# Mixture-of-slots layer: the dispatch product in two 64-token row tiles that also move an identity

## Chip, cores and metric

One core of a Trainium2 chip. The time is device microseconds of one execution of the program, as the median over several runs. The engines are TensorE (PE; its weight loads are PEld), VectorE (DVE), ScalarE (ACT), GpSimd (POOL) and SyncE (SP), which here only issues transfers.

## The reference, cut to what matters

The input x is 32 sequences of 64 tokens of 256 numbers. A cross attention (32 heads of 8) is added to x first. Then comes the part that is changed, a soft mixture of 16 experts with 128 slots each. The reference computes it as:

```python
x_ln = (x - mean) / jnp.sqrt(var + LN_EPS) * gamma + beta
x_n = _l2norm(x_ln, -1) * scale
logits = jnp.einsum('bnd,des->bnes', x_n, mu_n)
dispatch = jax.nn.softmax(logits, axis=1)
combine = jax.nn.softmax(logits.reshape(B, N, E * S), axis=-1)
slot_in = jnp.einsum('bnd,bnes->besd', x_ln, dispatch)
h = gelu(jnp.einsum('besd,edh->besh', slot_in, W1) + b1[None, :, None, :])
slot_out = jnp.einsum('besh,ehd->besd', h, W2) + b2[None, :, None, :]
out = jnp.einsum('bsd,bns->bnd', slot_out.reshape(B, E * S, D), combine)
```

Everything is float32.

## The kernel before, in words

**Tiling.** The 2048 tokens are 16 tiles of 128 tokens, so a tile is two sequences (b = 0 on partitions 0 to 63, b = 1 on 64 to 127). The attention runs over all 16 tiles first, then the expert layer over all 16. Each engine has its own program, and they meet at semaphores: `wait_ge(sem, n)` waits until a counter has reached n, `then_inc` raises it. An engine works through its list strictly in the written order, so the order of the calls in `ffn_step` of each engine's block is the schedule. The last attention tiles and the first steps of the layer are written out by hand.

**One step of the expert layer, tile s.** The product with W1 is taken before the dispatch, on the tokens, since both are linear: xw = x_ln W1 + b1, 16 experts times 64 columns, with a column of ones for the sum of the exponentials. The calls on TensorE (`ffn_step`, L1168) are:

- `expand` (L1114): xw, 1024 columns in two banks, with split operands: `mm3` (L913) makes three products of float32r halves (lines L915 to L917), so all rows of slot logits, expand and contract carry these three lines. VectorE's `xw_copy` (L809) adds b1 and puts the two sequences at different columns of `xw`, the rest of which is zero: four additions on 64 partitions.
- `transpose_e` (L1123): 16 transposes of the exponentials `eb` (tokens x slots) into banks 6, 7, 0, 1. `eT_copy` moves them to `eT`: groups 0 and 2 on ScalarE (L542), groups 3 and 1 on VectorE (L819), for the last tile all four on ScalarE.
- `transpose_xl` (L1093): the next tile's normalised input. VectorE's `xlT_copy` (L802) splits it into two halves.
- `dispatch` (L1131): for each expert `eb.T @ xw`, a 128-row product with 2 x 65 columns. A float32 product is two passes in the trace. The experts go in six groups, `HG`, of three (the last of one), one bank each, three banks in turn (`HB`); group i + 3 waits until group i has been read. VectorE's `hidden` (L834) takes the reciprocal of the sums and multiplies.
- `slot_logits` (L1100) of tile s + 1, in four banks of 512 columns. ScalarE's `slot_exps` (L534) makes `eb` of them.
- `combine` (L1144): a small transpose of the sums of exponentials, then 32 products of 64 columns in two column tiles, Gelu'd hidden values times `eT`, in two halves. ScalarE's `gT_high` (L553) casts each half, and VectorE's `gT_low` (L848) subtracts to get the low half.
- `contract` (L1159): the product with W2, which waits for these. VectorE's `finish` (L856) scales, adds x, and the tile is stored.

**ScalarE's order** (`ffn_step`, L559): `eT_copy` of two groups, `gelus` (three activations on two groups each, L548), `slot_exps` of tile s + 1, `gT_high`, then the sum of squares of tile s + 2. Gelu and Exp have different activation tables, so each step has two table loads, which appear at the lines of the Gelu (L551) and of the Exp (L539).

**VectorE's order** (`ffn_step`, L864): `clamp`, `xw_copy`, `xlT_copy`, `hidden` with the copies of `eT`, `center` of tile s + 2, `gT_low`, `sums` of tile s + 1, `finish`.

GpSimd does the affine part of the normalisation and the row scales (L417, L424). Before the layer it fills the constant parts of `xw` (L407 to L411).

Of the kernel before, what the change touches and what calls it, by code (L numbers as in the profile page):

```python
# [14 lines left out]
F32 = mybir.dt.float32  # L15
# [5 lines left out]
P = 128  # L21
# [13 lines left out]
HC = HID + 1  # L35

# [8 lines left out]
def build(nc, x, ctx_in, pos, Wq, Wkv, Wout, bout, gamma, beta, mu, scale, W1, b1, W2, b2, out):  # L45
    ctx = ExitStack()
    with ctx:
# [67 lines left out]
        rh = sb("rh", P, EXPERTS, 2)  # L115
# [3 lines left out]
        bank = [ctx.enter_context(nc.psum_tensor(f"bank{i}", [P, BANK], F32)) for i in range(8)]  # L119
# [83 lines left out]
        xw_step = sem("xw_step")  # L203
# [3 lines left out]
        eT_filled = sem("eT_filled")  # L207
        eT_act = sem("eT_act")
        eT_dve = sem("eT_dve")
# [25 lines left out]
        PER = BANK // (2 * HC)  # L235
# [4 lines left out]
        LB = (0, 1, 2, 5)  # L240
        HB = (4, 5, 3)
# [17 lines left out]
        XW = EXPERTS * 2 * HC  # L259
        xw = w12f[:, 0:XW].rearrange("p (e c) -> p e c", c=2 * HC)  # L260
# [3 lines left out]
        xl = xc  # L264

# [53 lines left out]
        def _(pool):  # L319
# [131 lines left out]
        def _(act):  # L451
# [101 lines left out]
            def gT_high(t):  # L553
                for c in range(2):
                    act.wait_ge(g_filled, t * 2 + c + 1)
                    a.copy(gT[0][:, 4 * c:4 * c + 4, :].rearrange("p a b -> p (a b)"), bank[(6, 3)[c]][:])\  # L556
# [28 lines left out]
        def _(dve):  # L585
# [216 lines left out]
            def xlT_copy(t):  # L802
                dve.wait_ge(xlT_filled, t + 1)
                v.tensor_copy(flat(xlT[0]), bank[2][:, 0:DIM]).then_inc(xlT_split, 1)
                dve.wait_ge(xlT_split, t + 1)
                v.tensor_tensor(flat(xlT[1]), bank[2][:, 0:DIM], flat(xlT[0]).bitcast(F32), ALU.subtract)\  # L806
# [12 lines left out]
            def eT_copy(t, gr):  # L819
                dve.wait_ge(eT_filled, t * 4 + gr + 1)  # L820
                v.tensor_copy(eT[:, 4 * gr:4 * gr + 4, :].rearrange("p a b -> p (a b)"), bank[(6, 7, 0, 1)[gr]][:])\
                    .then_inc(eT_dve, 1)
# [11 lines left out]
            def hidden(t, last):  # L834

                for i, gr in enumerate(HG):
                    if i == 3 and not last:
                        eT_copy(t, 3)
                    n, e0 = len(gr), gr[0]
                    dve.wait_ge(h_filled, t * len(HG) + i + 1)  # L840
                    src = bank[HB[i % 3]][:, 0:n * 2 * HC].rearrange("p (n b c) -> p n b c", b=2, c=HC)
                    v.reciprocal(rh[:, e0:e0 + n, :], src[:, :, :, HID]).then_inc(rh_done, 1)
                    dve.wait_ge(rh_done, t * len(HG) + i + 1)
                    v.tensor_tensor(hb[:, e0:e0 + n], src[:, :, :, 0:HID],  # L844
                                    rh[:, e0:e0 + n, :].unsqueeze(3).broadcast_to([P, n, 2, HID]),
                                    ALU.mult).then_inc(hn_ready, 1)

            def gT_low(t):  # L848
                dve.wait_ge(esT_filled, t + 1)
                v.tensor_copy(esT[:], bank[7][0:EXPERTS, 0:P]).then_inc(esT_ready, 1)  # L850
                for c in range(2):
                    high, low = (h[:, 4 * c:4 * c + 4, :].rearrange("p a b -> p (a b)") for h in gT)
                    dve.wait_ge(gT_split, t * 2 + c + 1)
                    v.tensor_tensor(low, bank[(6, 3)[c]][:], high.bitcast(F32), ALU.subtract).then_inc(gT_ready, 1)  # L854
# [9 lines left out]
            def ffn_step(s, p, last=False, ahead=True):  # L864
# [5 lines left out]
                hidden(s, last)  # L870
                if not last:
                    eT_copy(s, 1)
# [17 lines left out]
            residual(TILES - 2, 3)  # L890
            dve.wait_ge(wb_loaded, 64)
            dve.wait_ge(xw_const, 2)
# [16 lines left out]
        def _(pe):  # L909
# [183 lines left out]
            def transpose_xl(t, p):  # L1093
                pe.wait_ge(xl_ready, t + 1)
                wait(pe, xw_ready, t * 4 - 2)
                for k in range(KD):
                    m = nc.tensor.transpose(bank[2][:, k * P:(k + 1) * P], xl[:, p, k * P:(k + 1) * P], ident[:])
# [16 lines left out]
            def expand(t):  # L1114

                pe.wait_ge(e_ready, t * 4 + 3)
# [6 lines left out]
            def transpose_e(t):  # L1123
                for gr in range(4):
                    pe.wait_ge(e_ready, t * 4 + gr + 1)
                    for i in range(4):
# [108 lines left out]
```

## Time and profile before

| | |
|---|---|
| Median of 3 runs | 569.59 us |
| Runs | 567.27 to 569.8 us |
| Span of the profiled execution | 560.9 us |
| TensorE busy | 501.4 us, 89% |
| TensorE weight loads | 406.3 us, 72% |
| VectorE busy | 422.3 us, 75% |
| ScalarE busy | 290.3 us, 52% |
| GpSimd busy | 148.5 us, 26% |

The profiled execution has no time of its own beside its span; the runs lie 6.4 to 8.9 us above that span, which is what surrounds the first and last recorded instruction. In the page, busy shares are averages over an attention half (to about 245 us) and an expert half (from there on). A row of a timeline has a start, a length in us, the engine, the line, the operation and the tiles out<-in; a number in square brackets is the idle time of the engine just before, with what ended it.

### The profile page before, as it was taken

What the parts mean: (1) busy time and instruction counts of PE and PEld (TensorE: products, weight loads), DVE (VectorE), ACT (ScalarE), POOL (GpSimd) and SP (SyncE); (2) the same over time, 40 slices, a digit from 0 to 9 for tenths busy, and PEclk for the clock granted to TensorE, in tenths of its full rate; (3) what the DMA queues carried; (4) which work ended last, traced back from release to release, by engine and by line L of the source; (5) the groups of instructions that cost most, each with busy time, mean ns of one, the idle gap of its engine ahead of it and who ended that gap; (6) DMA issues with size and microseconds to landing.
All of it is one profiled execution on the core that took longest, in us unless ns stands there. A gap on an engine that the chain in (4) does not pass through costs nothing.

```text
span 560.9 us, 14312 instructions
## 1 busy us (share of the span) xinstructions
PE 501.4 (89%) x5544; PEld 406.3 (72%) x5544; DVE 422.3 (75%) x823; ACT 290.3 (52%) x537; POOL 148.5 (26%) x248
## 2 busy tenths in 40 slices
PE   0676999987797878889999999999999999999997
PEld 0444666654565555668888898898889889888986
DVE  5788998896799999856866686686668668666854
ACT  1363656664354646635455635745563574556344
POOL 4329211518363832311211212111121211112100
PEclk9868999999698989999999999999999999999999
DMA  6500000006000200000000000000000000000000
GB/s 188 197 6 6 8 6 7 8 1 160 6 6 5 62 0 1 4 1 1 11 11 2 11 9 9 0 9 9 0 9 9 9 0 9 9 0 9 11 11 11
DMA packets 15665, 11.65 MB, mean 21 GB/s; under 512 B 7040, under 2 KB 15120, under 8 KB 15376
## 3 DMA queue, kind: packets, MB, share of 16 engines
q1 hardware_dynamic: 15632, 11.18, 6.7%
q8 instruction: 25, 0.41, 0.3%
q14 instruction: 8, 0.07, 0.0%
HBM read 9.08 MB, written 2.10 MB: 20 GB/s over the span
## 4 chain that ended last, share of the span: by engine, by line
PE 75%; DVE 16%; ACT 3%; issue 2%; SPq 1%; DMA 1%; POOL 0%; DVEq 0%; ACTq 0%
PE bank L915 13%; PE bank L917 12%; PE bank L916 12%; PE bank L1140 10%; PE bank L1155 6%; PE bank L1127 5%; DVE qkr L664 4%; PE bank L965 4%; PE bank L980 4%; PE bank L994 3%; DVE rc L694 3%; PE bank L1014 2%; DVE mx L677 2%; PE bank L1161 2%; DVE pb L682 2%
## 5 line engine op out<-in xcount | busy, mean ns | idle before, releaser
L462 ACT ACTIVATE pb<-pb 128x512 f32<-128x512 f32 x64 | 39.4, 632 | 64.2 <-DVE pb L682 64.2
L545 ACT COPY mu_raw<-bank 128x512 f32<-128x512 f32 x34 | 19.7, 588 | 98.4 <-PE bank L1127 98.4
L1140 PE MATMUL bank<-w_raw,eb 128*128 128x130 f32 x512 | 60.2, 275 | 1.0 <-DVE w_raw L815 0.9
L1140 PEld LDWEIGHTS bank<-w_raw,eb 128*128 128x128 f32 x512 | 58.5, 190 | 1.5 <-DVE w_raw L815 1.4
L551 ACT ACTIVATE pb<-pb 128x768 f32<-128x768 f32 (+1 forms) x48 | 37.1, 774 | 40.1 <-DVE pb L844 40.1
L915 PE MATMUL bank<-mun_h,xlT_l 128*128 128x512 f32 x128 | 51.9, 405 | 0.2 <-DVE xlT_l L806 0.2
L844 DVE TENSOR_TENSOR pb<-bank,rh 128x384 f32<-128x384 f32 x96 | 49.3, 513 | 3.3
L980 PEld LDWEIGHTS bank<-ident,pb 128*128 128x128 f32 x256 | 31.3, 156 | 27.7 <-issue 25.0
L980 PE MATMUL bank<-ident,pb 128*128 128x128 f32 x256 | 45.9, 309 | 5.8 <-ACT vb L479 3.6
L917 PE MATMUL bank<-mun_h,xlT_h 128*128 128x512 f32 x128 | 50.6, 395 | 0.0
L916 PE MATMUL bank<-mun_l,xlT_h 128*128 128x512 f32 x128 | 50.5, 395 | 0.0
L815 DVE TENSOR_TENSOR w_raw<-bank,mu_raw 64x512 f32<-64x512 f32 x64 | 44.1, 689 | 6.4 <-PE bank L917 4.9
L677 DVE TENSOR_REDUCE mx<-bank 128x8 f32<-128x512 f32 x64 | 41.0, 682 | 9.3 <-PE bank L965 9.2
L539 ACT ACTIVATE eb<-bank,nshift,rn 128x512 f32<-128x512 f32 x64 | 44.9, 777 | 3.2 <-PE bank L917 1.6
L965 PE MATMUL bank<-kT,qT 32*64 32x256 f32 x512 | 45.1, 443 | 0.0
L854 DVE TENSOR_TENSOR gT_l<-bank,gT_h 128x512 fp32r<-128x512 f32 x32 | 22.1, 692 | 26.8 <-ACT gT_h L556 26.8
L420 POOL TENSOR_TENSOR xc<-xc,mu_raw 128x256 f32<-128x256 f32 x16 | 11.8, 735 | 115.0 <-DVE xc L792 115.0
L334 POOL TENSOR_TENSOR sm<-sm,mhalf 128x1 f32<-128x1 f32 x16 | 8.8, 549 | 123.6 <-DVE sm L799 123.6
L682 DVE TENSOR_TENSOR pb<-bank,mx 128x512 f32<-128x512 f32 x64 | 40.9, 679 | 0.0
L466 ACT COPY pT<-bank 128x512 f32<-128x512 f32 x64 | 35.7, 594 | 7.9 <-PE bank L980 7.7
L850 DVE COPY esT<-bank 16x128 f32<-16x128 f32 x16 | 4.4, 278 | 45.8 <-PE bank L1148 45.8
L915 PE MATMUL bank<-w_h,gT_l 128*128 128x256 f32 x128 | 37.1, 290 | 0.0
(156 smaller groups left out, 1261.2 us busy)
## 6 DMA issues: line engine op xcount, KB each, us to landing
mu_raw<-in_L_ffn_mu SPq DMA_DIRECT2D x1, 2048.0 KB, 12.8
out<-w_raw SPq DMA_DIRECT2D x16, 128.0 KB, 1.7
xa<-in_x SPq DMA_DIRECT2D x1, 1536.0 KB, 8.4
ctile<-in_ctx SPq DMA_DIRECT2D x16, 64.0 KB, 1.9
w_raw<-in_L_ffn_W SPq DMA_DIRECT2D x2, 512.0 KB, 5.3
w_raw<-in_L_ffn_W SPq DMA_DIRECT2D x1, 1024.0 KB, 9.1
xa<-in_x SPq DMA_DIRECT2D x1, 512.0 KB, 3.6
mu_raw<-in_L_ffn_b SPq DMA_DIRECT2D x1, 512.0 KB, 3.1
```

The source lines that it names most:

```text
L462: a.activation(pb[:, p, gr], pb[:, p, gr], ACT.Exp, scale=HD ** -0.5).then_inc(p_ready, 1)
L539: a.activation(eb[:, 4 * c:4 * c + 4, :].rearrange("p a b -> p (a b)"), bank[LB[c]][:], ACT.Exp, scale=rn[:, p:p + 1], bias=nshift[:]).the ...
L677: v.reduce_max(mx[:, gr, :], bank[gr][:].rearrange("p (h k) -> p h k", k=SEQ), AX.X)\
L682: v.tensor_tensor(pb[:, p, gr], bank[gr][:].rearrange("p (h k) -> p h k", k=SEQ), mx[:, gr, :].unsqueeze(2).broadcast_to([P, 8, SEQ]), ALU ...
L815: v.tensor_tensor(xw[rows, 8 * c:8 * c + 8, b * HC:b * HC + HID], bank[2 + c][rows].rearrange("p (e h) -> p e h", h=HID), b1b[rows, 8 * c: ...
L844: v.tensor_tensor(hb[:, e0:e0 + n], src[:, :, :, 0:HID], rh[:, e0:e0 + n, :].unsqueeze(3).broadcast_to([P, n, 2, HID]), ALU.mult).then_inc ...
L915: mm(o, a[1], b[0], start=first, stop=False)
L916: mm(o, a[0], b[1], start=False, stop=False)
L917: return mm(o, a[0], b[0], start=False, stop=last)
L965: m = mm(bank[g][cols, 256 * half:256 * half + 256].rearrange("p (j n) -> p j n", j=4), qT[rows, half, cols], kT[rows, half, :, cols], sta ...
L980: m = nc.tensor.transpose(bank[6 + gr % 2][:, i * P:(i + 1) * P], pb[:, p, gr, 2 * i:2 * i + 2, :].rearrange("p h k -> p (h k)"), ident[:])
L1140: m = mm(bank[HB[i % 3]][:, n * 2 * HC:(n + 1) * 2 * HC], eb[:, e, :], xw[:, e, :], start=True, stop=True)
```

## The change

The identity is put beside the 65 columns of each expert: `xw` becomes 16 x 129 columns, where row t holds xw, a one, and a one at column t of its own sequence. The dispatch of an expert becomes two products of 64 rows each, one for each sequence, into two neighbouring banks: columns 0 to 64 give the hidden sums, columns 65 to 128 the transposed exponentials. `transpose_e` and its copies go. ScalarE copies the transposed part of each group (six copies of up to 384 elements), and VectorE reads the rest of the pair of banks after it. The banks of the slot logits, of the next tile's transposes and of combine move with that, and so do some waits. `PER` is still 3, so there are six groups as before.

```diff
-        rh = sb("rh", P, EXPERTS, 2)
+        rh = sb("rh", P, 2, EXPERTS)
-        PER = BANK // (2 * HC)
+        PER = BANK // XC
-        LB = (0, 1, 2, 5)
-        HB = (4, 5, 3)
+        LB = (2, 3, 0, 1)
+
+        HB = (6, 4, 0)
+        def pair(i, n):
+
+            b0 = HB[i % 3]
+            return psum[:, b0:b0 + 2, 0:n * XC].rearrange("p b (n c) -> p b n c", c=XC)
...
@@ GpSimd
-            g.memset(w12f[:, 0:XW], 0.0).then_inc(xw_step, 1)
-            pool.wait_ge(xw_step, 1)
+            g.memset(xw[:, :, HID:HC], 1.0).then_inc(xw_const, 1)
             for b in range(2):
-                g.memset(xw[64 * b:64 * b + 64, :, b * HC + HID:b * HC + HC], 1.0).then_inc(xw_const, 1)
-            pool.wait_ge(xw_const, 2)
+                pool.wait_ge(xw_const, b + 1)
+                rows = slice(64 * b, 64 * b + 64)
+                g.tensor_copy(xw[rows, :, HC:XC], ident[rows, rows].unsqueeze(1).broadcast_to([64, EXPERTS, SEQ]))\
+                    .then_inc(xw_const, 1)
+            pool.wait_ge(xw_const, 3)
...
@@ ScalarE
-            def eT_copy(t, groups):
-                for gr in groups:
-                    act.wait_ge(eT_filled, t * 4 + gr + 1)
-                    a.copy(eT[:, 4 * gr:4 * gr + 4, :].rearrange("p a b -> p (a b)"),
-                           bank[(6, 7, 0, 1)[gr]][:]).then_inc(eT_act, 1)
+            def eT_copy(t):
+
+                for i, gr in enumerate(HG):
+                    n, e0 = len(gr), gr[0]
+                    act.wait_ge(h_filled, t * len(HG) + i + 1)
+                    a.copy(eT[:, e0:e0 + n, :].rearrange("p n (b k) -> p b n k", b=2),
+                           pair(i, n)[:, :, :, HC:XC]).then_inc(eT_ready, 1)
             def ffn_step(s, p, last=False, sums=True):
-                eT_copy(s, range(4) if last else (0, 2))
+                eT_copy(s)
                 gelus(s)
...
@@ VectorE
                 for c in range(2):
                     dve.wait_ge(xw_filled, t * 2 + c + 1)
-                    for b in range(2):
-                        rows = slice(64 * b, 64 * b + 64)
-                        v.tensor_tensor(xw[rows, 8 * c:8 * c + 8, b * HC:b * HC + HID],
-                                        bank[2 + c][rows].rearrange("p (e h) -> p e h", h=HID),
-                                        b1b[rows, 8 * c:8 * c + 8, :], ALU.add).then_inc(xw_ready, 1)
+                    v.tensor_tensor(xw[:, 8 * c:8 * c + 8, 0:HID], bank[2 + c].rearrange("p (e h) -> p e h", h=HID),
+                                    b1b[:, 8 * c:8 * c + 8, :], ALU.add).then_inc(xw_ready, 1)
-            def hidden(t, last):
+            def hidden(t):
                 for i, gr in enumerate(HG):
-                    if i == 3 and not last:
-                        eT_copy(t, 3)
                     n, e0 = len(gr), gr[0]
-                    dve.wait_ge(h_filled, t * len(HG) + i + 1)
+                    dve.wait_ge(eT_ready, t * len(HG) + i + 1)
+                    src = pair(i, n)
...
@@ TensorE
-            def dispatch(t):
-
-                pe.wait_ge(xw_ready, t * 4 + 4)
+            def dispatch(t, last, first=False):
+
+                pe.wait_ge(xw_ready, t * 2 + 2)
                 for i, gr in enumerate(HG):
-                    if i == 0:
+                    if i == 1:
                         wait(pe, yo_ready, t)
+                        if first:
+                            pe.wait_ge(x1_ready, TILES)
+                    if i == 2:
+                        pe.wait_ge(e_ready, t * 4 + 4)
+                        if not last:
+                            pe.wait_ge(xlT_ready, t + 2)
                     if i >= 3:
                         pe.wait_ge(hn_ready, t * len(HG) + i - 2)
                     for n, e in enumerate(gr):
-                        m = mm(bank[HB[i % 3]][:, n * 2 * HC:(n + 1) * 2 * HC], eb[:, e, :], xw[:, e, :],
-                               start=True, stop=True)
+                        for b in range(2):
+                            rows = slice(64 * b, 64 * b + 64)
+                            m = mm(bank[HB[i % 3] + b][:, n * XC:(n + 1) * XC], eb[rows, e, :], xw[rows, e, :],
+                                   start=True, stop=True)
                     m.then_inc(h_filled, 1)
...
@@ slot_logits: the waits
-                    if c < 2:
-                        wait(pe, (eT_act, eT_dve)[c], (t * 2, t * 2 - 1)[c])
-                    elif c == 3:
-                        wait(pe, hn_ready, (t - 1) * len(HG) + 5)
+                    if c == 2:
+                        wait(pe, hn_ready, t * len(HG))
@@ combine: the waits
                 pe.wait_ge(es_ready, t + 1)
-                pe.wait_ge(eT_act, t * 2 + (4 if last else 2))
-                pe.wait_ge(eT_dve, t * 2 + (0 if last else 2))
+                pe.wait_ge(hn_ready, t * len(HG) + len(HG))
@@ ffn_step
                 if not expanded:
                     expand(s)
-                transpose_e(s)
-                if expanded:
-                    pe.wait_ge(x1_ready, TILES)
                 if not last:
                     transpose_xl(s + 1, 1 - p)
-                dispatch(s)
+                dispatch(s, last, first=expanded)
```

In `expand` the wait for the Exps of the tile is now for two of them instead of three, in `transpose_xl` it is for all four, and `xlT_copy` reads bank 1.

## Rows read from the trace of the kernel before

**Rows 1.** The page: busy time by engine, and the chain that ended last, by engine.
```profile
PE 501.4 (89%) x5544; PEld 406.3 (72%) x5544; DVE 422.3 (75%) x823; ACT 290.3 (52%) x537; POOL 148.5 (26%) x248
...
PE 75%; DVE 16%; ACT 3%; issue 2%; SPq 1%; DMA 1%; POOL 0%; DVEq 0%; ACTq 0%
```

**Rows 2.** The chain in order of time: start, us, what (dispatch of four tiles).
```profile
253.29 3.85 PE bank L1140 x32
...
273.20 3.85 PE bank L1140 x32
...
293.08 3.58 PE bank L1140 x32
...
528.44 3.58 PE bank L1140 x32
```

**Rows 3.** Timeline, TensorE, 405 to 423 us: start, us, engine, line, op, out<-in.
```profile
405.84 0.39 PE L915 MATMUL bank<-w_h,xlT_l 128*128 128x512 f32 x1
...
408.63 1.91 PE L1127 MATMUL bank<-ident,eb 128*128 128x128 f32 x16
...
410.38 0.38 PE L1097 MATMUL bank<-ident,xc 128*128 128x128 f32 x2
...
410.60 3.75 PE L1140 MATMUL bank<-w_raw,eb 128*128 128x130 f32 x32
...
414.10 0.48 PE L915 MATMUL bank<-mun_h,xlT_l 128*128 128x512 f32 x1
...
419.98 2.09 PE L1155 MATMUL bank<-mu_raw,pb 128*64 128x64 f32 x64
...
422.62 0.38 PE L915 MATMUL bank<-w_h,gT_l 128*128 128x256 f32 x1
```

**Rows 4.** Timeline, ScalarE, the same step.
```profile
410.75 1.28 ACT L551 ACT_TABLE_LOAD   x1
...
413.11 0.84 ACT L551 ACTIVATE pb<-pb 128x768 f32<-128x768 f32 x1 [1.07 <-DVE pb L844]
...
416.19 0.63 ACT L551 ACTIVATE pb<-pb 128x512 f32<-128x512 f32 x1 [0.25 <-DVE pb L844]
...
416.84 1.28 ACT L539 ACT_TABLE_LOAD   x1
...
418.13 2.79 ACT L539 ACTIVATE eb<-bank,nshift,rn 128x512 f32<-128x512 f32 x4
...
421.18 0.59 ACT L556 CAST gT_h<-bank 128x512 fp32r<-128x512 f32 x1 [0.26 <-PE bank L1155]
```

**Rows 5.** Timeline, VectorE, the same step.
```profile
407.43 2.85 DVE L815 TENSOR_TENSOR w_raw<-bank,mu_raw 64x512 f32<-64x512 f32 x4 [0.24 <-PE bank L917]
...
412.29 0.19 DVE L842 RECIPROCAL rh<-bank 128x6 f32<-128x6 f32 x1
...
412.51 0.56 DVE L844 TENSOR_TENSOR pb<-bank,rh 128x384 f32<-128x384 f32 x1
...
412.99 0.18 DVE L842 RECIPROCAL rh<-bank 128x6 f32<-128x6 f32 x1
...
421.80 0.69 DVE L854 TENSOR_TENSOR gT_l<-bank,gT_h 128x512 fp32r<-128x512 f32 x1 [1.43 <-ACT gT_h L556]
```

**Rows 6.** Line L493: count, ns min/median/max, first and last start.
```profile
L493 ACT CAST xT_h<-bank x16: 479/484/485, 14.3 to 212.3; 128x384 fp32r<-128x384 f32 x16
```

**Rows 7.** Timeline, TensorE, one group of attention logits.
```profile
203.31 0.66 PE L965 MATMUL bank<-kT,qT 32*64 32x256 f32 x8
```

**Rows 8.** Timeline of the last tile, TensorE and VectorE.
```profile
547.67 3.81 PE L1140 MATMUL bank<-w_raw,eb 128*128 128x130 f32 x32
...
548.61 0.20 DVE L842 RECIPROCAL rh<-bank 128x6 f32<-128x6 f32 x1 [1.03 <-PE bank L1140]
...
552.41 2.08 PE L1155 MATMUL bank<-mu_raw,pb 128*64 128x64 f32 x64 [0.82 <-ACT pb L551]
```

**Rows 9.** Timeline, VectorE, before the first dispatch.
```profile
250.39 2.84 DVE L815 TENSOR_TENSOR w_raw<-bank,mu_raw 64x512 f32<-64x512 f32 x4
```

More of the change, by code:

```diff
@@ L35 @@
 HC = HID + 1
+XC = HC + SEQ
 def wait(eng, sem, value):
@@ L114, in build @@
         rs = sb("rs", P, 2, 2)
-        rh = sb("rh", P, EXPERTS, 2)
+        rh = sb("rh", P, 2, EXPERTS)
         gT = split("gT", P, EXPERTS // 2, P)
         esT = sb("esT", EXPERTS, P)
-        bank = [ctx.enter_context(nc.psum_tensor(f"bank{i}", [P, BANK], F32)) for i in range(8)]
+        psum = ctx.enter_context(nc.psum_tensor("psum", [P, 8, BANK], F32))
+        bank = [psum[:, i, :] for i in range(8)]
         x_loaded = [sem("x_loaded0"), sem("x_loaded1")]
@@ L258, in build @@
         w12f = flat(w12_raw)
-        XW = EXPERTS * 2 * HC
-        xw = w12f[:, 0:XW].rearrange("p (e c) -> p e c", c=2 * HC)
+        XW = EXPERTS * XC
+        xw = w12f[:, 0:XW].rearrange("p (e c) -> p e c", c=XC)
         yo = w12f[:, XW:XW + 2 * DIM].rearrange("p (a d) -> p a d", d=DIM)
@@ L555, in gT_high @@
                     act.wait_ge(g_filled, t * 2 + c + 1)
-                    a.copy(gT[0][:, 4 * c:4 * c + 4, :].rearrange("p a b -> p (a b)"), bank[(6, 3)[c]][:])\
+                    a.copy(gT[0][:, 4 * c:4 * c + 4, :].rearrange("p a b -> p (a b)"), bank[6 + c][:])\
                         .then_inc(gT_split, 1)
             def ffn_step(s, p, last=False, sums=True):
-                eT_copy(s, range(4) if last else (0, 2))
+                eT_copy(s)
                 gelus(s)
@@ L853, in gT_low @@
                     dve.wait_ge(gT_split, t * 2 + c + 1)
-                    v.tensor_tensor(low, bank[(6, 3)[c]][:], high.bitcast(F32), ALU.subtract).then_inc(gT_ready, 1)
+                    v.tensor_tensor(low, bank[6 + c][:], high.bitcast(F32), ALU.subtract).then_inc(gT_ready, 1)
             def finish(t, p):
@@ L869, in ffn_step @@
                     xlT_copy(s + 1)
-                hidden(s, last)
-                if not last:
-                    eT_copy(s, 1)
+                hidden(s)
                 if ahead:
@@ L889, in _ @@
             normalise(TILES - 2)
-            residual(TILES - 2, 3)
+            residual(TILES - 2)
             dve.wait_ge(wb_loaded, 64)
-            dve.wait_ge(xw_const, 2)
+            dve.wait_ge(xw_const, 3)
             sums(0, 0)
@@ L1094, in transpose_xl @@
                 pe.wait_ge(xl_ready, t + 1)
-                wait(pe, xw_ready, t * 4 - 2)
+                wait(pe, e_ready, t * 4)
                 for k in range(KD):
-                    m = nc.tensor.transpose(bank[2][:, k * P:(k + 1) * P], xl[:, p, k * P:(k + 1) * P], ident[:])
+                    m = nc.tensor.transpose(bank[1][:, k * P:(k + 1) * P], xl[:, p, k * P:(k + 1) * P], ident[:])
                 m.then_inc(xlT_filled, 1)
@@ L1121, in expand @@
                     m.then_inc(xw_filled, 1)
[L1123 to L1126, printed above, removed]
-                        m = nc.tensor.transpose(bank[(6, 7, 0, 1)[gr]][:, i * P:(i + 1) * P], eb[:, 4 * gr + i, :],
-                                                ident[:])
-                    m.then_inc(eT_filled, 1)
-            def dispatch(t):
-                pe.wait_ge(xw_ready, t * 4 + 4)
+            def dispatch(t, last, first=False):
+                pe.wait_ge(xw_ready, t * 2 + 2)
                 for i, gr in enumerate(HG):
-                    if i == 0:
+                    if i == 1:
                         wait(pe, yo_ready, t)
+                        if first:
[4 more added lines that the diff above has]
+                            pe.wait_ge(xlT_ready, t + 2)
                     if i >= 3:
@@ L1139, in dispatch, with combine @@
                     for n, e in enumerate(gr):
-                        m = mm(bank[HB[i % 3]][:, n * 2 * HC:(n + 1) * 2 * HC], eb[:, e, :], xw[:, e, :],
-                               start=True, stop=True)
+                        for b in range(2):
+                            rows = slice(64 * b, 64 * b + 64)
+                            m = mm(bank[HB[i % 3] + b][:, n * XC:(n + 1) * XC], eb[rows, e, :], xw[rows, e, :],
+                                   start=True, stop=True)
                     m.then_inc(h_filled, 1)
-            def combine(t, last):
+            def combine(t):
                 pe.wait_ge(es_ready, t + 1)
-                pe.wait_ge(eT_act, t * 2 + (4 if last else 2))
-                pe.wait_ge(eT_dve, t * 2 + (0 if last else 2))
-                nc.tensor.transpose(bank[7][0:EXPERTS, 0:P], es[:], ident[:]).then_inc(esT_filled, 1)
+                pe.wait_ge(hn_ready, t * len(HG) + len(HG))
+                nc.tensor.transpose(bank[5][0:EXPERTS, 0:P], es[:], ident[:]).then_inc(esT_filled, 1)
                 for c in range(2):
@@ L1170, in ffn_step @@
                     expand(s)
-                transpose_e(s)
-                if expanded:
-                    pe.wait_ge(x1_ready, TILES)
                 if not last:
                     transpose_xl(s + 1, 1 - p)
-                dispatch(s)
+                dispatch(s, last, first=expanded)
                 if not last:
                     slot_logits(s + 1)
-                combine(s, last)
+                combine(s)
                 contract(s)
```

29 lines of the change are left out of this document (10 added, 19 removed).

## The prediction, made before the changed kernel was run

> **What bounds the kernel now.** I read the page first. TensorE is busy for 89% of the span and carries 75% of the chain that ended last [rows 1]: less work on TensorE is worth something, unless the order of the other engines takes its place. The chain in order of time then gives the pace of the second half: the dispatch product of a tile starts every (528.44 − 293.08) / 12 = 19.61 us [rows 2]. The question is what sets these 19.61 us after the change.
>
> The timeline of one step on TensorE [rows 3], counted from the start S of the dispatch (410.60), reads: dispatch 3.50, slot logits of the next tile and the small transpose to 9.38, combine, contract from 12.02 (422.62), expand from 14.85 (405.84 plus a period) to 17.64 (408.63 plus a period), then 1.97 us of transposes, 16 of the exponentials and 2 of the next tile, until the next dispatch. There is hardly a gap: TensorE sets the pace.
>
> ScalarE beside it [rows 4] is what I would have the reader look at. Its order is fixed: copies of transposed exponentials, Gelu table, three Gelus, Exp table, four Exps, then the casts of the combined product. The Gelu table is loaded at S + 0.15, while the engine waits for its first input, which comes at S + 2.51. The last Exp ends at S + 10.32 (418.13 + 2.79), and the first cast starts at S + 10.58: the whole queue has 0.26 us to spare. VectorE [rows 5] follows each cast with a subtraction, and TensorE's contract starts 0.13 us after the first of those.
>
> Times here are of the profiled execution, span 560.9. The median of the runs is 569.59, 8.7 us more; I add my difference to it. About 0.5% (2.8 us) is what a measurement can tell from no change.
>
> **The change, part by part.** Removed on TensorE: 16 transposes a tile. They take 410.60 − 408.63 less 0.22 for the two that stay, 1.75 us a step [rows 3]; if nothing else moved, 28 us in 16 steps.
>
> Their cover is lost. While they ran, VectorE added the bias for the dispatch (four 64-partition additions, 2.85 us, 0.71 each [rows 5], the last ending 0.32 before the dispatch). Now there are two additions on 128 partitions. The width in partitions should cost nothing, since the row of 384 elements on 128 partitions takes 0.56; I take 0.70 for each. The second begins 0.24 after expand's end, as the third of the four does now, so the dispatch starts at 0.24 + 0.70 + 0.06 = 1.00 us after expand, not 1.97. The 0.06 is from 253.23, where the additions of the first tile end, to 253.29 [rows 2, 9]. Of the 1.75 us, 0.97 are left.
>
> The dispatch itself: 32 passes of 130 columns took 3.50, 0.109 each [rows 3]. Now each expert has two 64-row products of 129 columns, four passes, in two banks. The trace has no 64-row tile. The nearest row is the 32-row, 64-column product: eight passes of 256 columns in 0.66 us [rows 7], where eight in series at the rate of the dispatch would take 1.7. Combine, in two column tiles, shows it too: 64 passes of 64 columns in 2.09 [rows 3], in series 3.4. So tiles run side by side. Lower bound 0.107 for a pair of passes, upper bound 0.22 (in series); I take 0.112, near the rows with tiles. A group of three experts: 0.67.
>
> The ordering now costs: ScalarE copies the transposed half of each pair of banks first, and only then may VectorE take the reciprocals and multiply. A group is seen by its reader 0.94 after its first pass (548.61 − 547.67) [rows 8]. The copy has 384 elements of two banks; a cast of 384 out of one took 0.48 [rows 6]; bounds 0.38 and 0.59, those of 256 and of 512 elements (the cast of 512 took 0.59, and the Gelus of 768 and 512 differ by 0.21 for 256 elements [rows 4]). Then reciprocal to product 0.22 and product 0.56, one group each 0.70 [rows 5]. From S: group 1 filled 0.94, copied 1.42, normalised 2.23; groups 2 and 3 at 2.93 and 3.63. There are three pairs of banks, so groups 4, 5, 6 start at 2.29, 2.99, 3.69. The last group is one expert: filled 4.18, its copy waits for that of group 5 (3.93 to 4.41) and ends at 4.57 (estimate: 0.48 less 0.21, so 0.27 for 128 elements). TensorE is done with the dispatch at 3.91 instead of 3.50; the stalls come from VectorE's 0.70 a group.
>
> Other waits that the change adds, taken at nothing: group 3 waits for the split of the next tile's transposed input (VectorE, two operations of 0.42 behind the bias additions, ready near S + 0.9, wanted at 1.34); the third slice of slot logits waits for the last normalised group (5.6, wanted at 6.8). Behind VectorE's new waits for ScalarE stand the centring of the tile after next and the subtractions; those are wanted at 12, and VectorE no longer has the two copies of 0.68. No DMA is issued in another order.
>
> Now ScalarE's queue, which is the point of my forecast. All six copies stand before the Gelus. The table load, which used to fall into the wait, comes behind the last copy: 4.59 to 5.87. Gelus (0.84, 0.84, 0.63, each beginning 0.11 before the other ends, as the four Exps in 2.79 do) 5.88 to 7.98. Table 8.00 to 9.28. Exps to 12.07 in full, the last starting at 11.30, and the first cast can start at 11.96. Subtraction 12.58 to 13.27 and contract at 13.40, where it is 12.02 now: **+1.38**. TensorE has combined half a tile by 3.91 + 0.1 + 5.88 + 1.20 = 11.09, so it waits.
>
> Sum of a step: 13.40 + contract 2.83 + expand 2.79 + 1.00 = **20.02 against 19.61, +0.41**.
>
> Rule against row: each table load in the trace takes 1.28 and the first Exp starts 0.01 behind it (416.84, 418.13) [rows 4]. The Trainium skill, page "ScalarE: Activation LUTs", section "What ACT_TABLE_LOAD costs", counts a drain of about 1.38 us on top for every switch. The trace of before does not show it, neither at the Exp load (which begins 0.02 behind the last Gelu) nor behind it. By the page, both switches now being exposed, the step would be some 2.8 us longer, near 22.8; I go by the row.
>
> At the front: two additions of 0.71 fewer before the first dispatch [rows 9], −1.4; the first step, which also has the variances of the last tiles on VectorE, goes from 19.91 (253.29 to 273.20) [rows 2] to about 20.1, +0.2. On GpSimd one memset of 2080 columns is replaced by one of 16 and two copies of the identity, long before the first dispatch; bound ±0.5, hidden by the attention tiles, taken as 0. Then 14 steps (273.20 to 547.67) of +0.41: +5.7. At the end combine starts at the end of the second Gelu plus 0.06, at 7.51, where it is 552.41 − 547.67 = 4.74 after the dispatch [rows 8]: +2.8. Sum −1.4 + 0.2 + 5.7 + 2.8 = +7.3: span 568.2, **time 576.9**.
>
> **The rivals.** (a) *Faster, 0.12.* The Gelu table is loaded ahead of the copies, where ScalarE idles, as the copies need no table of their own. Price: 1.28 off ScalarE's chain. It decides as soon as the chain is more than 0.87 (11.96 − 11.09) shorter: then TensorE sets the pace again at 20.02 − 0.87 = 19.15 a step. 15 × −0.46, −1.4 at the front, +2.8 − 1.28 at the end: −6.8, 562.8. Against it: in [rows 4] the load stands behind the copies, right in front of the Gelus.
>
> (b) *No difference, 0.20.* ScalarE's chain is 0.3 to 0.6 shorter than I have it (copies at 0.42, quicker releases, more overlap between Gelus): 570 ± 2.5. The step's two losses then just eat the 0.97.
>
> (c) *Tiles in series, 0.05.* Each expert takes four passes, 0.45 us; a group 1.34, so the last copy ends near 7.70, not 4.57. +3.1 a step, about 627. The rows of tiled products speak against it. The Trainium skill, page "TensorE: Matmul & The Clock Gate", section "LDWEIGHTS (loading the stationary operand)", has a load cost by its columns and not its rows: that gives four full loads an expert where there were two, and would bring this case if loads of different row tiles did not overlap. In the row at 203.31 eight loads and products fit in 0.66.
>
> (d) The forecast, ScalarE's queue as the bound: 0.63, 573 to 582.
>
> **The numbers.** Slower is (d) and (c), 0.68; same 0.20; faster 0.12. The likeliest case gives 576.9. The low end takes in (a), 562; the high end the bounds above: copies at 0.59 with a slower release (+0.2 a step) and pairs of passes at 0.12 (+0.1), 584. Case (c) is left out. The likeliest case alone: 573 to 582.
>
> **What would show it.** Right: no row for the transposes; a dispatch of about 3.9 us with short idles on VectorE's products; period near 20.0; Gelu table load at S + 4.6; the first cast following the last Exp with no idle, and TensorE idle for about 1.1 us before contract "until VectorE's subtraction", and about 0.8 before the dispatch, until the bias addition. Wrong: a Gelu load before S + 1 (case a); idle of ScalarE before the cast on TensorE (b or a); dispatch passes 0.11 apart one by one, 7 us in all (c); a gap between a table load and its neighbours (the page's drain).

## The result and the profile after

The changed kernel took 577.08 us (median of 4 runs, 574.23 to 578.23), the kernel before 568.43 beside it, a ratio of 1.0137 with a 95% interval of 1.0094 to 1.018. A second series gave 578.01 against 567.82, ratio 1.0201 (1.0172 to 1.023). The ratios and intervals are the ones on record; they need not equal the quotient of two medians (here 1.0152 and 1.0179). The change is slower by 1.4 to 2%.

The spans of the two profiles differ by more (576.0 against 560.9) than the medians do. Most of the excess lies ahead of the part that was changed: in the first profile of the kernel before, the attention ran with a mean granted clock of 0.93, in the profile after with 0.91, and the first dispatch came 3.6 us later where 1.4 us earlier was predicted. Experiment 5 comes back to this. One sentence on the time before was wrong: the 6.4 to 8.9 us between that profile's span and the runs are not only what surrounds the recorded instructions. In the eleven profiled executions since, whose own times are on record, the time is 1.8 to 2.4 us above the span (578.23 over 576.0 here). By that the first profile caught an execution of some 563 us (an estimate), faster than any of the runs beside it.

The page after, busy time and the chain that ended last, which answer to [rows 1]:

```profile
PE 494.7 (86%) x5800; PEld 389.4 (68%) x5800; DVE 383.8 (67%) x761; ACT 305.1 (53%) x599; POOL 149.0 (26%) x248
...
PE 46%; ACT 22%; DVE 21%; issue 8%; SPq 1%; DMA 1%; POOL 0%; ACTq 0%; DVEq 0%
```

TensorE has lost 6.7 us of busy time: 10.5 in the expert half (303.9 to 293.5), while the attention half at its lower clock took 3.7 more (197.5 to 201.2). The chain that ended last is now only 46% TensorE; ScalarE, 3% before, has 22%. The bound has moved. The chain in order of time (start, us, what), which answers to [rows 2]:

```profile
256.84 0.96 PE psum L1135 x12
...
276.95 0.96 PE psum L1135 x12
...
558.35 0.96 PE psum L1135 x12
```

The period is (558.35 − 276.95) / 14 = 20.10 us, where it was 19.61. One step on TensorE, as in [rows 3]: start, us, engine, line, op, and in brackets the idle time before and what ended it.

```profile
417.60 4.22 PE L1135 MATMUL psum<-w_raw,eb 64*128 64x129 f32 x64 [0.57 <-DVE w_raw L822]
421.75 0.50 PE L912 MATMUL psum<-mun_h,xlT_l 128*128 128x512 f32 x1
...
427.65 2.08 PE L1149 MATMUL psum<-mu_raw,pb 128*64 128x64 f32 x64
...
431.03 0.39 PE L912 MATMUL psum<-w_h,gT_l 128*128 128x256 f32 x1 [0.67 <-DVE gT_l L853]
...
433.97 0.40 PE L912 MATMUL psum<-w_h,xlT_l 128*128 128x512 f32 x1
...
436.76 0.38 PE L1094 MATMUL psum<-ident,xc 128*128 128x128 f32 x2
437.71 0.49 PE L1135 MATMUL psum<-w_raw,eb 64*128 64x129 f32 x4 [0.56 <-DVE w_raw L822]
```

Here 417.60 is the start S of the dispatch. It lasts to 421.75, 4.15 us. The two gaps are the ones to read: 0.67 us before contract, until VectorE's subtraction (beside the weight load's own wait of 1.1), and 0.56 before the next dispatch, until the bias addition. ScalarE in the same step, as in [rows 4]:

```profile
418.58 0.48 ACT L554 COPY mu_raw<-psum 128x384 f32<-128x384 f32 x1 [7.55 <-PE psum L1135]
...
421.62 0.65 ACT L554 COPY mu_raw<-psum 128x384 f32<-128x384 f32 x2 [0.21 <-PE psum L1135]
422.29 1.28 ACT L560 ACT_TABLE_LOAD   x1
423.58 2.10 ACT L560 ACTIVATE pb<-pb 128x768 f32<-128x768 f32 x3
425.70 1.28 ACT L546 ACT_TABLE_LOAD   x1
427.00 2.79 ACT L546 ACTIVATE eb<-psum,nshift,rn 128x512 f32<-128x512 f32 x4
429.66 1.08 ACT L565 CAST gT_h<-psum 128x512 fp32r<-128x512 f32 x2
```

From 421.62 to the end of the casts there is no idle time at all: the last two of the six copies, table, Gelus, table, Exps, casts. In [rows 4] the Gelus and the cast that are shown had an idle time in brackets; now none has. VectorE, as in [rows 5]:

```profile
430.29 1.29 DVE L853 TENSOR_TENSOR gT_l<-psum,gT_h 128x512 fp32r<-128x512 f32 x2 [2.25 <-ACT gT_h L565]
...
436.96 0.69 DVE L822 TENSOR_TENSOR w_raw<-psum,mu_raw 128x512 f32<-128x512 f32 x1 [0.70 <-PE psum L914]
```

The subtraction now waits 2.25 us for a cast, not 1.43. The second bias addition (436.96, 128 partitions) takes 0.69, like one of 64 partitions before, and starts 0.20 after expand's end.

### The profile page after: what moved, and what is told of

Read it like the earlier page. It is cut to its first block, busy times and chain, and to the rows that moved or that the text cites. A ratio compares the mean times of both kernels' runs of the same rounds, so it can differ in the third digit from the quotient of the medians.

```text
span 576.0 us, 14783 instructions
## 1 busy us (share of the span) xinstructions
PE 494.7 (86%) x5800; PEld 389.4 (68%) x5800; DVE 383.8 (67%) x761; ACT 305.1 (53%) x599; POOL 149.0 (26%) x248
## 4 chain that ended last, share of the span: by engine, by line
PE 46%; ACT 22%; DVE 21%; issue 8%; SPq 1%; DMA 1%; POOL 0%; ACTq 0%; DVEq 0%
PE psum L912 8%; PE psum L1135 7%; ACT eb L546 7%; PE psum L914 7%; PE psum L913 7%; PE psum L962 4%; PE psum L977 4%; DVE qkr L673 4%; ACT pb L560 4%; PE psum L991 3%; ACT L560 3%; DVE rc L703 3%; ACT mu_raw L554 2%; DVE w_raw L822 2%; PE psum L1011 2%
## 5 line engine op out<-in xcount | busy, mean ns | idle before, releaser
L554 ACT COPY mu_raw<-psum 128x384 f32<-128x384 f32 x96 | 41.0, 445 | 141.0 <-PE psum L1135 141.0
L1135 PE MATMUL psum<-w_raw,eb 64*128 64x129 f32 x1024 | 66.6, 279 | 11.6 <-DVE w_raw L822 10.7
L1135 PEld LDWEIGHTS psum<-w_raw,eb 64*128 64x128 f32 x1024 | 60.4, 187 | 18.7 <-DVE w_raw L822 14.7
L912 PE MATMUL psum<-mun_h,xlT_l 128*128 128x512 f32 x128 | 52.2, 408 | 0.2 <-DVE xlT_l L815 0.2
L977 PE MATMUL psum<-ident,pb 128*128 128x128 f32 x256 | 47.0, 314 | 6.1 <-ACT vb L486 3.8
L843 DVE TENSOR_TENSOR pb<-psum,rh 128x384 f32<-128x384 f32 x96 | 49.2, 513 | 3.3
L914 PE MATMUL psum<-mun_h,xlT_h 128*128 128x512 f32 x128 | 50.6, 395 | 0.0
L913 PE MATMUL psum<-mun_l,xlT_h 128*128 128x512 f32 x128 | 50.5, 395 | 0.0
L546 ACT ACTIVATE eb<-psum,nshift,rn 128x512 f32<-128x512 f32 x64 | 44.9, 777 | 3.3 <-PE psum L914 1.6
L962 PE MATMUL psum<-kT,qT 32*64 32x256 f32 x512 | 46.4, 454 | 0.0
```

Of the source, the lines that this page charges most:

```text
L546: a.activation(eb[:, 4 * c:4 * c + 4, :].rearrange("p a b -> p (a b)"), bank[LB[c]][:], ACT.Exp, scale=rn[:, p:p + 1], bias=nshift[:]).the ...
L554: a.copy(eT[:, e0:e0 + n, :].rearrange("p n (b k) -> p b n k", b=2), pair(i, n)[:, :, :, HC:XC]).then_inc(eT_ready, 1)
L843: v.tensor_tensor(hb[:, e0:e0 + n].rearrange("p n b h -> p b n h"), src[:, :, :, 0:HID], rh[:, :, e0:e0 + n].unsqueeze(3).broadcast_to([P, ...
L912: mm(o, a[1], b[0], start=first, stop=False)
L913: mm(o, a[0], b[1], start=False, stop=False)
L914: return mm(o, a[0], b[0], start=False, stop=last)
```

## The experiments

Edits are against the changed kernel unless another is named. Periods are taken between the starts of the dispatches of tiles 1 and 15; S is the start of a dispatch. All runs of a kernel stand beside runs of the kernel before on the same chip.

| | time | before | ratio (interval) | period | last dispatch to end |
|---|---|---|---|---|---|
| before, first profile | 569.59 | | | 19.61 | 13.2 |
| changed | 577.08 | 568.43 | 1.0137 (1.0094 to 1.018) | 20.10 | 17.6 |
| 1 Gelu table early | 564.07 | 568.05 | 0.9896 (0.9852 to 0.9941) | 19.28 | 14.7 |
| 2 dispatch on one half | 567.24 | 568.05 | 0.9975 (0.9944 to 1.0006) | 19.45 | 17.4 |
| 3 both | 552.0 | 568.05 | 0.968 (0.9628 to 0.9732) | 18.74 | 14.8 |
| 4 more TensorE work | 577.11 | 568.05 | 1.014 (1.0066 to 1.0215) | 20.08 | 17.7 |
| 5 before again | 565.58 | | one run | 19.61 | 13.3 |
| 6 tiles in turn | 589.33 | | one run | 20.70 | 18.4 |
| 7 more ScalarE work | 584.71 | 570.16 | 1.0277 (1.0223 to 1.033) | 20.49 | 18.1 |
| 8 kept busy at the end | 582.9 | 570.16 | 1.0232 (1.0172 to 1.0292) | 20.11 | 16.1 |
| 9 changed again | 578.01 | 567.82 | 1.0201 (1.0172 to 1.023) | 20.08 | 17.8 |
| 10 as 8 | 574.48 | 567.82 | 1.0176 (1.0099 to 1.0252) | 20.07 | 16.2 |

### 1. The Gelu table ahead of the copies

```diff
+        early = sb("early", P, 1)
...
+                a.activation(early[:], nshift[:], ACT.Gelu)
                 eT_copy(s)
                 gelus(s)
```

> One Gelu of a single column is issued before the six copies of each step, so that its table is loaded while ScalarE idles. My theory (ScalarE's queue of six copies, table load, three Gelus, table load, four Exps sets the step): the queue gets 1.28 us shorter, TensorE's combine is the next limit after 0.81 us (first cast at S + 12.06, half a tile combined at 10.05 + 1.20 = 11.25), so the period goes from 20.11 to about 19.3, and the last tile gains 1.3: some 13 us, near 564. Rival 1 (the cost is the cover lost for the bias additions before the dispatch): ScalarE has slack, the period stays 20.1, 577. Rival 2 (the table load can't be moved, or costs a drain where it stands): 577 or more.

Measured 564.07, period 19.28. ScalarE and TensorE of one step (S = 413.14):

```profile
417.17 0.65 ACT L555 COPY mu_raw<-psum 128x384 f32<-128x384 f32 x2 [0.22 <-PE psum L1137]
417.70 2.11 ACT L561 ACTIVATE pb<-pb 128x768 f32<-128x768 f32 x3
419.83 1.28 ACT L547 ACT_TABLE_LOAD   x1
...
424.40 0.59 ACT L566 CAST gT_h<-psum 128x512 fp32r<-128x512 f32 x1 [0.42 <-PE psum L1151]
...
426.35 1.28 ACT L570 ACT_TABLE_LOAD   x1
```

```profile
413.14 4.22 PE L1137 MATMUL psum<-w_raw,eb 64*128 64x129 f32 x64 [0.57 <-DVE w_raw L824]
...
423.20 2.09 PE L1151 MATMUL psum<-mu_raw,pb 128*64 128x64 f32 x64
```

The Gelus follow the last copy with no load between them, the load has moved to 426.35 where ScalarE idles, and the first cast (424.40) now waits 0.42 us for TensorE's combine, as it did before the change. The gain is 0.82 a step although 1.28 was taken off the queue: the rest is TensorE's own limit. Rival 1 and rival 2 are out.

The last tile gained more than the 1.3 us that I expected: from its dispatch to the end it took 14.7 us, not 17.6.

```profile
553.89 0.27 PE L1144 MATMUL psum<-ident,es 128*16 128x128 f32 x1 [1.65 <-DVE pb L845]
554.21 2.08 PE L1151 MATMUL psum<-mu_raw,pb 128*64 128x64 f32 x64
```

The idle time of 1.47 us in front of combine is gone, which brings combine 1.4 us forward, and the granted clock stays at 1.00, so combine takes 2.08 us where the changed kernel took 3.56. Experiments 8 to 10 are about this clock.

### 2. The dispatch waits for half of the bias additions

```diff
-                pe.wait_ge(xw_ready, t * 2 + 2)
+                pe.wait_ge(xw_ready, t * 2 + 1)
...
                     if i == 2:
+                        pe.wait_ge(xw_ready, t * 2 + 2)
                         pe.wait_ge(e_ready, t * 4 + 4)
```

> The dispatch waits for the first bias addition only (experts 0 to 7); the second is waited for before group 3. My theory: ScalarE's queue hangs on the start of the dispatch, so an earlier start shortens the step in full: 0.70 us earlier, 0.1 to 0.2 lost again as group 3 then waits for VectorE's split of the next input; period 19.5, about 567. Rival (the start of the dispatch is not on the path, since ScalarE has been bounded elsewhere): no change, 577.

Measured 567.24, period 19.45. TensorE:

```profile
417.62 4.34 PE L1136 MATMUL psum<-w_raw,eb 64*128 64x129 f32 x64
...
431.05 0.39 PE L912 MATMUL psum<-w_h,gT_l 128*128 128x256 f32 x1 [0.55 <-DVE gT_l L853]
```

The dispatch has no idle time in front of it any more and takes 0.1 us more (4.34). The wait before contract is still there, and it is still 13.43 from S (431.05 − 417.62): ScalarE's queue is unchanged and only starts sooner. So the wait for the second addition costs 0.65 a step, and it is paid because the start of the dispatch also starts ScalarE's queue. The execution that was profiled took 573.3 us, 6 more than the median: its clock ahead of the first dispatch was 0.89, and it fell again at the first dispatch (5.59 us long). The period and the step above lie behind that, at a clock of 1.00.

### 3. Both

Both edits together.

> Both edits. My theory: the gains add, as the first shortens ScalarE's queue down to TensorE's limit and the second moves the start of both: period 20.11 - 0.81 - 0.6 = 18.7, about 554 to 555, below the kernel before. Rival 1 (only the lost cover counts): as the second edit alone. If the two shared one path they would not add, and the result would be near the better one of the two, 564.

Measured 552.0, period 18.74, ratio to the kernel before 0.968: both parts of the gain are kept, and this is faster than both kernels by 16 and 25 us. Page and one step:

```profile
PE 493.4 (89%) x5800; PEld 388.9 (70%) x5800; DVE 386.0 (70%) x761; ACT 311.3 (56%) x615; POOL 149.0 (27%) x248
```

```profile
407.86 4.34 PE L1138 MATMUL psum<-w_raw,eb 64*128 64x129 f32 x64
...
418.04 2.09 PE L1152 MATMUL psum<-mu_raw,pb 128*64 128x64 f32 x64
...
426.61 1.61 PE L1138 MATMUL psum<-w_raw,eb 64*128 64x129 f32 x24
```

```profile
412.42 2.11 ACT L561 ACTIVATE pb<-pb 128x768 f32<-128x768 f32 x3
...
419.23 0.59 ACT L566 CAST gT_h<-psum 128x512 fp32r<-128x512 f32 x1 [0.42 <-PE psum L1152]
```

TensorE is busy for 89% of a span of 553.7 us and sets the pace again; the cast waits for it.

### 4. More work on TensorE

```diff
+                for _ in range(5):
+                    nc.tensor.transpose(bank[5][0:EXPERTS, 0:P], es[:], ident[:])
                 nc.tensor.transpose(bank[5][0:EXPERTS, 0:P], es[:], ident[:]).then_inc(esT_filled, 1)
```

> Five more small transposes (0.109 us each, 0.55 us a step) before combine. My theory: TensorE has 0.81 us to spare there, as it waits for the casts anyway: no change, 577, and the wait before contract shrinks from 0.67 to about 0.1. Rival (TensorE's own work still sets the pace): +0.55 a step, 8 us, 585.

Measured 577.11, period 20.08: five more transposes a step cost nothing.

```profile
416.54 4.22 PE L1135 MATMUL psum<-w_raw,eb 64*128 64x129 f32 x64 [0.56 <-DVE w_raw L822]
...
426.38 0.71 PE L1143 MATMUL psum<-ident,es 128*16 128x128 f32 x5
```

In this profile the transposes are there (426.38), the period is the same, and in place of the 0.67 us before contract no idle time of TensorE is listed; its weight loads there wait 0.54 us where they waited 1.07.

### 7. More work on ScalarE

```diff
+        spare = sb("spare", P, 3 * P)
...
                 eT_copy(s)
+                a.copy(spare[:], wqkv[0][:, 0:2, :].rearrange("p a b -> p (a b)")[:, 0:3 * P].bitcast(F32))
                 gelus(s)
```

> One more ScalarE copy of 384 elements between the copies and the Gelus of each step (0.5 us, some 0.4 after overlap). My theory: ScalarE's queue is the path from dispatch to contract, so all of it is paid: +0.4 a step, 6.5 us, near 583.5. Rival (TensorE or the bias additions set the pace): no change, 577.

Measured 584.71, period 20.49, +0.39. The copy took 0.53 and pushed all that follows (S = 419.80 here):

```profile
424.36 0.53 ACT L571 COPY spare<-wqkv_h 128x384 f32<-128x384 f32 x1
424.89 1.28 ACT L561 ACT_TABLE_LOAD   x1
...
432.26 1.08 ACT L566 CAST gT_h<-psum 128x512 fp32r<-128x512 f32 x2
```

```profile
433.64 0.39 PE L914 MATMUL psum<-w_h,gT_l 128*128 128x256 f32 x1 [1.06 <-DVE gT_l L855]
```

Contract starts at S + 13.84 instead of 13.43, and TensorE waits 1.06 us instead of 0.67. Experiments 4 and 7 are the two sides of one question: 0.55 us on TensorE are free, 0.4 us on ScalarE are paid in full.

### 6. Row tiles in turn

```diff
-                    for n, e in enumerate(gr):
-                        for b in range(2):
+                    for b in range(2):
+                        for n, e in enumerate(gr):
                             rows = slice(64 * b, 64 * b + 64)
```

> The three experts of a group in the first row tile, then the same three in the second, so that neighbouring products share a tile. If products run side by side only when neighbours lie in different row tiles, a group takes twelve passes of 0.11 = 1.3 us, not 0.67, the last copy ends 3.1 us later, the period is about 23.2, the time about 627: this is what the change would have cost with tiles in series. If the hardware overlaps them in any order, or they were not side by side before, the period stays 20.1.

Measured 589.33 in one run, period 20.70. Neither outcome: the order costs 0.6 us a step, not 3.1. One step (S = 424.16):

```profile
424.16 4.84 PE L1135 MATMUL psum<-w_raw,eb 64*128 64x129 f32 x64 [0.56 <-DVE w_raw L822]
```

```profile
425.46 0.48 ACT L554 COPY mu_raw<-psum 128x384 f32<-128x384 f32 x1 [7.76 <-PE psum L1135]
426.14 0.48 ACT L554 COPY mu_raw<-psum 128x384 f32<-128x384 f32 x1 [0.19 <-PE psum L1135]
...
428.12 0.48 ACT L554 COPY mu_raw<-psum 128x384 f32<-128x384 f32 x1 [0.83 <-PE psum L1135]
```

The first copy comes at S + 1.30 instead of 0.98, but the second follows 0.68 later, so groups still fill at the pace of pairs. In the records the first pass in the second tile starts 0.33 us after the first in the first tile, when only three of the six passes written ahead of it have started, and the rest goes in pairs, the second tile's with the next group's in the first. (The rows don't name the row tile. That the pass at 0.33 is of the second one is read from its length of 0.37 us and the 0.21 to its next, which only a first pass shows, and from the group ending at 1.27.) So what the description of the kernel says of every engine, that it works strictly in the written order, does not hold for the starts of TensorE's passes in different row tiles. The loss is 0.3 us at the first group and 0.3 at the fourth (ScalarE waits 0.83 for it, against 0.52). So what the change would cost with tiles wholly in series was not brought about by this edit and stays untried.

### 5. The kernel before, again

> The kernel before, unchanged, for a second profile. In the first, TensorE's clock was at the lower level for 34 us ahead of the first dispatch, in the profiles of the changed kernel and its variants for 44 to 55 us, and their first dispatch comes 2.6 to 7.4 us later, although it should come 1.4 us earlier. If that is chance of the execution, a second profile of the kernel before may show 40 to 50 us at the lower level and a first dispatch near 258; the period stays 19.61. If the change causes it (its waits or GpSimd's new fill in the attention part), it shows 34 us and 253.3 again.

```profile
0.00:256.12 256.12, 200.86 (x2768) 142.17 (x2768) 212.01 (x367) 129.84 (x307) 103.50 (x116) 0.91 0.13 37
```

```profile
0.00:256.84 256.84, 201.20 (x2752) 142.36 (x2752) 211.50 (x365) 127.61 (x304) 103.05 (x113) 0.91 0.13 37
```

These are the stretches ahead of the first dispatch, of this run and then of the changed kernel (us, busy us of PE, PEld, DVE, ACT and POOL, granted clock, DMA share, GB/s). The kernel before, unchanged, had a first dispatch at 256.12 and a clock of 0.91 this time, against 253.29 and 0.93, with 44 us at the lower level instead of 34, and its period was 19.61 again. In all profiles, the variants' too, this stretch is between 251.9 (clock 0.93) and 261.0 (0.89) us long. So several us of the difference between two profiles are the clock of the attention part, which the change doesn't touch. Profiles at the same clock can be compared: at 0.93, experiment 10's first dispatch came at 251.85 and the kernel before's at 253.29, the 1.4 us earlier of the prediction, and the last attention projection at 248.52 and 248.40. So that pair shows no effect of the change on the attention itself. At 0.91 the changed kernel had 255.90 and 256.84 against the 256.12 here, where 254.7 would be 1.4 earlier; an effect of one or two us, or the clock falling at other moments, can't be told apart there.

### 8 to 10. TensorE kept busy in the last tile

```diff
-            def combine(t):
+            def combine(t, last=False):
                 pe.wait_ge(es_ready, t + 1)
+                if last:
+                    for _ in range(16):
+                        nc.tensor.transpose(bank[3][0:EXPERTS, 0:P], es[:], ident[:])
...
+                if last:
+                    for _ in range(12):
+                        nc.tensor.transpose(bank[3][0:EXPERTS, 0:P], es[:], ident[:])
                 for c in range(2):
```

> In the last tile only, 28 redundant small transposes fill TensorE's two waits before combine (1.65 and 1.47 us). In the changed kernel the clock is at the lower level for 3.4 us there and combine takes 3.56 us, not 2.09. If the idle time lowers the clock, the fill keeps it up: combine 2.1 us, from the last dispatch to the end 16.2 us, not 17.6, so 1.4 us off the total, which only the profile can show. If the clock falls for another reason, combine stays at 3.5 and the end at 17.6.

> The changed kernel once more, beside the next run. Period 20.1, last dispatch to end 17.6, time 577; what moves is the start of the first dispatch, with the time at the lower clock ahead of it.

> The fill in the last tile once more. It gave 582.9 where I expected 575.7, although the last tile took the 16.1 us I expected: the excess lay ahead (first dispatch at 261.0, first step 22.5 us with 6.8 us at the lower clock in it). If that was chance of two executions, the time is now about 1.4 below the changed kernel's, near 575.7, with a first step of 20.1. If it belongs to this program, it is 583 again with the same low stretch at 260 us.

The last tile of the changed kernel, and of the kernel with the fill (experiment 10):

```profile
558.35 4.22 PE L1135 MATMUL psum<-w_raw,eb 64*128 64x129 f32 x64 [0.79 <-DVE w_raw L822]
564.22 0.27 PE L1142 MATMUL psum<-ident,es 128*16 128x128 f32 x1 [1.65 <-DVE pb L843]
565.96 3.56 PE L1149 MATMUL psum<-mu_raw,pb 128*64 128x64 f32 x64 [1.47 <-ACT pb L560]
```

```profile
555.41 4.22 PE L1135 MATMUL psum<-w_raw,eb 64*128 64x129 f32 x64 [0.78 <-DVE w_raw L822]
559.56 1.91 PE L1143 MATMUL psum<-ident,es 128*16 128x128 f32 x16
...
561.42 1.47 PE L1148 MATMUL psum<-ident,es 128*16 128x128 f32 x12
563.02 2.08 PE L1155 MATMUL psum<-mu_raw,pb 128*64 128x64 f32 x64
```

After idle times of 1.65 and 1.47 us combine took 3.56 us; with them filled it took 2.08. The granted clock of that stretch says why:

```profile
566.00:570.00 4.00, 4.00 (x66) 3.66 (x66) 0.69 (x1) 1.46 (x3) 0.00 (x0) 0.57 0.00 0
```

0.57 is mostly the lower level (1.2 GHz); with the fill it was 1.00 to the end in experiment 10. The last tile gained 1.5 us, where 1.4 was expected. Experiment 1 agrees: the idle time of 1.65 us stood there alone, and the clock stayed at 1.00. The first series of this kernel nevertheless gave 582.9 us and the second 574.48 (573.49 to 582.41), 3.5 below the changed kernel beside it. The difference lies in front: in both profiles of it the clock fell at the first dispatch, where TensorE waits 2.01 us for the bias additions. Its first dispatch in experiment 10:

```profile
251.85 6.64 PE L1135 MATMUL psum<-w_raw,eb 64*128 64x129 f32 x64 [2.01 <-DVE w_raw L822]
```

It took 6.64 us instead of 4.22 (6.61 in experiment 8), and the first step 22.56 instead of 20.1. In both profiles of the changed kernel, and in those of experiments 1, 4, 6 and 7, the same wait of 2.01 us was there without this; in experiment 2 it happened after a wait of 1.41, and in experiment 3, after the same 1.41, it did not. The fill stands in the last tile only, so I know of no way in which it could act on the first, but two out of two with it and none out of six without it is not settled. The totals of 8 and 10 bear on the fill only within several us; the 1.5 us of the profile is what it is worth. Between 8 and 10 themselves lies the attention: the first dispatch came at 261.0 with a clock of 0.89 in one and at 251.9 with 0.93 in the other, the same program both times. Why an execution gets the one or the other stays open.

## Why the prediction was right

The step that carried it was ScalarE's queue, and the schedule held point by point. From S, predicted and measured:

| | predicted | after |
|---|---|---|
| first group copied from | 0.94 | 0.98 |
| dispatch ends | 3.91 | 4.15 |
| last copy ends | 4.57 | 4.67 |
| Gelu table load | 4.59 | 4.69 |
| Exp table load | 8.00 | 8.10 |
| first Exp | 9.30 | 9.40 |
| casts from | 11.96 | 12.06 |
| contract | 13.40 | 13.43 |
| contract itself | 2.83 | 2.94 |
| expand | 2.79 | 2.79 |
| expand to next dispatch | 1.00 | 0.95 |
| step | 20.02 | 20.10 |

One figure of the prediction does not add up: the first group was to be normalised at 2.23, and its own terms give 2.20 (1.42 + 0.22 + 0.56). It measured 2.29, and nothing else hangs on the 0.03.

**The removed transposes.** They were gone, and the 1.75 us was used up, with half a us more, mostly where it was said: 0.73 between expand and dispatch (0.95 against the 0.22 of the transposes that stay), 0.65 in the dispatch (4.15 − 3.50, predicted 0.41), 0.74 between combine and contract (3.38 against 2.64) and 0.11 in contract, together 2.23, which less 1.75 is 0.48, the 0.49 of the step within rounding. The 0.11 in contract was not foreseen. The dispatch is the term I had too small: a pass that starts after a wait takes 0.37 us in the records, not 0.27, and the next pair follows 0.21 later instead of 0.11. That happens at the start and again at group 4, which waits for VectorE; groups 5 and 6 also wait, but lose only some 0.02 each in this way (0.30 us, and 0.14 to the next pair).

**Row tiles.** They run side by side at 0.111 us a pair of passes (estimate 0.112). The premise of case (c) held, but not its conclusion: the weight loads of 64 rows take 0.187 us each in the mean, as much as those of 128 rows before (0.190), but the two of a pair start 0.007 us apart. Case (c) was priced too simply too: experiment 6 shows that even a bad order would have kept most of the overlap.

**Copies.** 0.48 for 384 elements from two banks, as the cast from one.

**Table loads.** The row won: 1.28 us each and no further drain, at 425.70 to 427.00 behind a Gelu and at 422.29 to 423.58 behind a copy, now that both loads are exposed. By the Trainium skill, page "ScalarE: Activation LUTs", section "What ACT_TABLE_LOAD costs", which adds a drain of about 1.38 us to every switch, the step would have been near 22.8 (an estimate); it was 20.10, so the measurement decides against the drain here.

**The sum.** At the front −1.4 was predicted; from TensorE's last attention projection to the first dispatch it is 4.89 before and 3.32 after, −1.57. The first step +0.2: 19.91 to 20.11. Fourteen steps +5.7: 14 × 0.495 = +6.9. The end +2.8: +4.4, for 1.5 us more came from the lower clock in combine, which I had not foreseen. Together +9.9 against +7.3; the medians give +8.65 and +10.2. So the sum was 2.6 us short: 1.6 at the end, 1.2 in the fourteen steps (0.08 each), less 0.2 at the front. That the absolute forecast of 576.9 lies so close to 577.08 is luck: the kernel before had a median of 568.4 beside the changed one and not the 569.6 that the forecast started from, and the time to the first dispatch varies from execution to execution by more than these terms. The stated range, 562 to 584, takes in no change and a gain as well; what tests the mechanism is the narrower 573 to 582 and the schedule above.

**Rival (a)** was the change that one would want: the load did not move by itself, but moved by hand it gave 564.07 (the rival's price was 562.8), by the mechanism and near the limit given for it: a step of 19.28, where the rival had 19.15.

## What to carry to other kernels

When work is removed from the engine that bounds, look at what was hidden behind it, and at the place in each other engine's queue where the replacement is put: here six copies put in front of three Gelus drew a table load of 1.28 us and the Exps of the next tile onto the path. A table load can be moved into idle time by a one-element activation of the coming function, and a wait for a whole operand can be cut to the part that is needed first; together they turned a loss of 1.4% into a gain of 3.2%. To know which engine sets a period, add half a microsecond to each in turn and see which one pays: here TensorE had 0.55 us to spare and ScalarE nothing.

## What the runs showed of the hardware

- Products of 64 rows and 128 columns, loads included, run two at a time in different row tiles (0.111 us for two passes of 129 columns). They still do so when they stand three products apart in the program, where products of the second tile start ahead of ones of the first that are written before them.
- The first pass after a wait took 0.1 us more than the next ones (0.37 against 0.27) and the next followed 0.1 later than usual, at the start of the dispatch and at its fourth group. At the two shorter waits behind it, it was 0.02.
- A TensorE idle of 1.65 and one of 1.47 us with little between them were followed by the lower clock level for most of 4 us (0.57 granted over 566 to 570), and 28 transposes in them prevented that; with the 1.65 alone (experiments 1 and 3) the clock stayed at 1.00. After one idle of 2.01 us ahead of the first dispatch it stayed up in six of eight profiles and fell in the two with the fill (first dispatch 4.22 and 6.64 us), so one such wait alone does not decide it.
- Attention ahead of the change ran at a granted clock of 0.89 to 0.93 from one execution to the next, worth some 9 us between the extremes (experiments 8 and 10, the same program), as much as the change itself.
